# First output stage of a two-layer attention kernel: low halves on GpSimd, and the second layer's moments taken per unit

## The reference, cut to what matters

```
x = x + _L0_conv_ref(_gn(x), registers, qkv_w, qkv_b, out_w, out_b)
x = x + _L1_conv_ref(_gn(x), qkv_w, qkv_b, proj_w, proj_b, rel_pos_h, rel_pos_w)
```

## Time and profile before

| what | value |
| --- | --- |
| median of 3 runs | 3226.82 us (3225.55 to 3229.48) |
| the profiled execution | 3222.15 us, its span 3220.3 us |
| mean granted TensorE clock | 0.957 of 2.4 GHz |
| PE busy | 2905.4 us, 90% |
| DVE busy | 2476.7 us, 77% |
| ACT busy | 1861.9 us, 58% |
| POOL busy | 1902.8 us, 59% |
| DMA | 301.91 MB, mean 94 GB/s |

### The profile page before, as it was taken

One profiled execution on the slowest core, in us unless ns is written; L12 is line 12 of the kernel. 1 busy time (PEld: TensorE's weight loads), 2 busy tenths in 40 slices (PEclk: granted clock), 3 DMA queues, 4 the chain that ended last, 5 costly groups with the idle time before them and its releaser, 6 DMA issues. The chain is left out here.

```text
span 3220.3 us, 82906 instructions
## 1 busy us (share of the span) xinstructions
PE 2905.4 (90%) x34200; PEld 1874.4 (58%) x34200; DVE 2476.7 (77%) x5171; ACT 1861.9 (58%) x3434; POOL 1902.8 (59%) x1561
## 2 busy tenths in 40 slices
PE   4996999997579885999999999999999999999977
PEld 2453677774335442666666666666666666666644
DVE  6754888885666534888888888888888888888854
ACT  3333676664344432666666666666666666666655
POOL 3452555552110123777777777777777777777762
PEclk9896999998789986999999999999999999999989
DMA  3326555555437658322222222222222233332115
GB/s 142 155 89 147 135 135 141 142 140 192 143 108 215 195 131 203 63 51 52 51 52 52 51 51 51 51 52 52 51 51 51 52 61 59 58 59 54 21 42 147
DMA packets 219836, 301.91 MB, mean 94 GB/s; under 512 B 134394, under 2 KB 172884, under 8 KB 213972
## 3 DMA queue, kind: packets, MB, share of 16 engines
q1 hardware_dynamic: 219460, 296.62, 37.7%
HBM read 196.56 MB, written 92.64 MB: 90 GB/s over the span
## 5 line engine op out<-in xcount | busy, mean ns | idle before, releaser
L1746 POOL TENSOR_TENSOR fprob_low<-fprob 128x768 f16<-128x768 f32 x1008 | 1449.2, 1468 | 445.2 <-ACT fprob L1714 445.2
L1757 DVE TENSOR_REDUCE fpart_max<-fmax_acc 128x1 f32<-128x384 f32 x2592 | 1354.0, 556 | 252.0 <-PE fmax_acc L1585 235.9
L1714 ACT ACTIVATE fprob<-fscores 128x768 f32<-128x768 f32 x1296 | 1049.3, 810 | 592.5 <-PE fscores L1614 592.4
L1585 PE MATMUL fmax_acc<-fk_m,fq_m 128*128 128x384 f16 x2592 | 847.8, 327 | 32.6 <-DMA fident<-in_ident 27.6
L1612 PE MATMUL fscores<-fq_a,fk_a 128*128 128x384 f16 x2592 | 843.0, 325 | 10.6 <-DMA fk_m<-in_one_m 10.6
L1614 PE MATMUL fscores<-fq_b,fk_b 97*128 97x384 f16 x2592 | 846.9, 327 | 0.0
L1638 PE MATMUL fout_acc<-fv,fprob 128*128 128x65 f16 x7776 | 609.4, 191 | 2.5 <-POOL fprob_low L1746 2.1
L1639 PE MATMUL fout_acc<-fv,fprob_low 128*128 128x33 f16 x7776 | 593.8, 179 | 0.0
L1638 PEld LDWEIGHTS fout_acc<-fv,fprob 128*128 128x128 bf16 x7776 | 541.6, 97 | 76.5 <-POOL fprob_low L1746 5.2
L1639 PEld LDWEIGHTS fout_acc<-fv,fprob_low 128*128 128x128 f16 x7776 | 485.6, 96 | 72.5
L1131 POOL TENSOR_TENSOR prob_low<-prob 128x242 f16<-128x242 f32 (+2 forms) x360 | 250.0, 717 | 254.7 <-ACT prob L1089 252.9
(11 more groups left out here) (134 smaller groups left out, 3980.5 us busy)
## 6 DMA issues: line engine op xcount, KB each, us to landing
q_a<-q_hi SPq DMA_DIRECT2D x48, 432.0 KB, 5.7
fq_a<-q_hi SPq DMA_DIRECT2D x48, 432.0 KB, 7.6
q_a<-q_lo SPq DMA_DIRECT2D x24, 432.0 KB, 7.5
row_bias<-bias_slot SPq DMA_DIRECT2D x24, 432.0 KB, 6.8
col_bias<-bias_slot SPq DMA_DIRECT2D x72, 144.0 KB, 4.7
fq_a<-q_lo SPq DMA_DIRECT2D x24, 432.0 KB, 8.6
fq_a<-col_bias SPq DMA_DIRECT2D x24, 432.0 KB, 16.8
fq_b<-row_bias SPq DMA_DIRECT2D x24, 432.0 KB, 5.8
```

Of the source, the lines that this page charges most:

```text
L1585: nc.tensor.matmul(max_acc[:, piece_bank(g, u, j), 0:PIECE], q_m[:, b, tile * 128:(tile + 1) * 128], k_m[:, b, piece * PIECE:(piece + 1) * ...
L1714: nc.scalar.activation(prob[:, k % RING, :].rearrange("p (j n) -> p j n", j=2), scores[:, 2 * (k % 2):2 * (k % 2) + 2, 0:UNIT], ACT.Exp).t ...
L1746: engine.tensor_tensor(prob_low[:, k % RING, :], prob[:, k % RING, :], prob[:, k % RING, :].bitcast(BF16)[:, 1::2], ALU.subtract).then_inc ...
L1757: nc.vector.reduce_max(part_max[:, u % 2, j // PIECES, j % PIECES:j % PIECES + 1], max_acc[:, piece_bank(g, u, j), 0:PIECE], axis=AX.X).th ...
```

## The change

In `mix`, `normed` gets two buffers, the low halves are issued by GpSimd, in a loop over the units behind its weight step, and `normalise` keeps the multiplication alone; it waits for the low halves of two units before in place of one. After the add of unit u VectorE takes the moments of unit u - 1 (three `bn_stats`, one for each tile), and at the end those of the last unit. The tensor `stats` is made in `build` and handed to both phases; `front` for layer 1 takes no moments of its own. The number and form of the moment instructions, and what they read, stay the same.

```
 def front(nc, ctx, x, values, stats, layer, dram, sem):
...
-            for i in range(CT * B):
-                t, b = i // B, i % B
-                if layer == 0:
+            if layer == 0:
+                for i in range(CT * B):
+                    t, b = i // B, i % B
                     dve.wait_ge(x_in[i], 16)
-                for a in range(NA):
-                    at = b * TOK + a * UNIT
-                    last = nc.vector.bn_stats(stats[:, i * NA + a, :], x[:, t, at:at + UNIT])
-            link(last)
+                    for a in range(NA):
+                        at = b * TOK + a * UNIT
+                        last = nc.vector.bn_stats(stats[:, i * NA + a, :], x[:, t, at:at + UNIT])
+                link(last)
...
 def mix(nc, ctx, x, stats, layer, dram, sem):
...
-    normed = ctx.enter_context(nc.sbuf_tensor(f"normed{layer}", [128, CT, UNIT], F32))
+    normed = ctx.enter_context(nc.sbuf_tensor(f"normed{layer}", [128, 2, CT, UNIT], F32))
...
         def _(pool):
             pool.wait_ge(w_steps, 2)
             nc.gpsimd.tensor_tensor(w_lo[:, :, :], w[:, :, :], w_hi[:, :, :], ALU.subtract).then_inc(w_lo_ready, 1)
+            for u in range(UNITS):
+                pool.wait_ge(normed_hi_ready, u + 1)
+                if u >= 2:
+                    pool.wait_ge(acc_ready, (u - 1) * CT)
+                nc.gpsimd.tensor_tensor(normed_lo[:, u % 2], normed[:, u % 2], normed_hi[:, u % 2],
+                                        ALU.subtract).then_inc(normed_lo_ready, 1)
...
                 dve.wait_ge(unit_in[u % 3], 32 * (u // 3 + 1))
                 dve.wait_ge(factor_ready, u + 1)
-                if u > 0:
-                    dve.wait_ge(normed_lo_ready, u)
-                nc.vector.tensor_tensor(normed[:, :, :], factor[:, 0:CT, 0:UNIT], heads[:, u % 3],
+                if u > 1:
+                    dve.wait_ge(normed_lo_ready, u - 1)
+                nc.vector.tensor_tensor(normed[:, u % 2], factor[:, 0:CT, 0:UNIT], heads[:, u % 3],
                                         ALU.mult).then_inc(normed_ready, 1)
-                dve.wait_ge(normed_hi_ready, u + 1)
-                if u >= 2:
-                    dve.wait_ge(acc_ready, (u - 1) * CT)
-                nc.vector.tensor_tensor(normed_lo[:, u % 2], normed[:, :, :], normed_hi[:, u % 2],
-                                        ALU.subtract).then_inc(normed_lo_ready, 1)
+
+            def moments(u):
+                dve.wait_ge(added, u + 1)
+                for t in range(CT):
+                    nc.vector.bn_stats(stats[:, t * UNITS + u, :], x[:, t, u * UNIT:(u + 1) * UNIT])
...
                 nc.vector.tensor_tensor(dst, mixed[:, u % 2], dst, ALU.add).then_inc(added, 1)
+                if u >= 1:
+                    moments(u - 1)
+            moments(UNITS - 1)
...
-                nc.scalar.activation(normed_hi[:, u % 2], normed[:, :, :], ACT.Identity).then_inc(normed_hi_ready, 1)
+                nc.scalar.activation(normed_hi[:, u % 2], normed[:, u % 2], ACT.Identity).then_inc(normed_hi_ready, 1)
...
         x = whole.enter_context(nc.sbuf_tensor("x", [128, CT, ALL + REGS], F32))
+        stats = whole.enter_context(nc.sbuf_tensor("stats", [128, CT * B * NA, 6], F32))
```

More of the change, by code:

```diff
@@ L133, in split_halves, with front @@
     return halves[:, 0::2], halves[:, 1::2]
-def front(nc, ctx, x, values, layer, dram, sem):
+def front(nc, ctx, x, values, stats, layer, dram, sem):
     regs = REGS if layer == 0 else 0
@@ L157, in front @@
     normed = ctx.enter_context(nc.sbuf_tensor(f"gn_out{layer}", [128, 3, THIRD], F32))
-    stats = ctx.enter_context(nc.sbuf_tensor(f"stats{layer}", [128, CT * B * NA, 6], F32))
     chan = ctx.enter_context(nc.sbuf_tensor(f"chan{layer}", [128, CT * B, 2], F32))
@@ L1216, in _, with mix @@
             each_stage(pool, stage)
-def mix(nc, ctx, x, layer, dram, sem):
+def mix(nc, ctx, x, stats, layer, dram, sem):
     w = ctx.enter_context(nc.sbuf_tensor(f"ow{layer}", [128, CT, C], F32))
@@ L2017, in build @@
             values = first.enter_context(nc.sbuf_tensor("values", [128, HEADS, B * TILES + 1, VW], F16))
-            phase(front, x, values, 0)
+            phase(front, x, values, stats, 0)
             phase(attention, x, values, 0)
-            phase(mix, x, 0)
-        phase(front, x, None, 1)
+            phase(mix, x, stats, 0)
+        phase(front, x, None, stats, 1)
         phase(attention_full, x)
```

## The result

The changed kernel's median is 3240.01 us (10 runs), that of the kernel before 3226.55 us (10 runs): 1.0041 times as long, with a 95% interval of 1.0032 to 1.0049. The prediction was 3238, slower, with 3229 to 3247 as its range.

A forecast was written before the change was run, and what follows sets the result against it. It took TensorE (5.15 of 5.27 us a unit) and VectorE's loop as nearly equal limits. Output stage +21.3 less front 10.2 gave +11.1 us, median 3226.82 to 3237.9 (forecast 3238), range 3229 to 3247.

The forecast's parts named there:

- The loop: First output stage, per unit: add 1.13, moments 1.39, normalise to low halves 2.58, low halves 2.37; 7.47 us against 5.27.
- The rival without a wait: Output stage: the add runs beside GpSimd at full speed, loop 6.66 us, net +3.9, 3230.7 us; 12 in 100.
- The length of the stage: First output stage: nine loops of 7.47 us bring unit 11's low halves 21.3 us later.
- The six moments behind the last add: End of the output stage: 2.8 us of moments, costed at nothing because the last store covers them.
- The front: Second layer's front: without the 16.65 us moment pass, first x low halves come 10.2 us earlier, held by GpSimd's weight low halves.
- The chain to the scale factors: Second layer's front: without the moment pass, ready 14.6 us after the stage's start, or later if the group matrix lands late.
- The sum: Whole kernel: +21.3 from the output stage less 10.2 from the front, +11.1 us.
- the lower clock as a rival: Output stage: waiting TensorE drops its clock; +8 us if every other unit fell, +18 if all nine; 10 in 100.
- as before: End of the output stage: the last add starts 5.21 us after unit 11's first matmul, unchanged.
- Without a gap of its own VectorE closes the loop: Output stage before the change: VectorE's steps follow directly, TensorE waits for low halves; nearly equal limit to TensorE's 5.15 of 5.27 us.
- The rival that called VectorE's free time usable: Output stage: units overlap until TensorE sets the pace at 5.15 us; -9.7 us, 3217; 8 in 100.

The follow-up runs named there:

- run 1: Changed kernel with the second layer's moments left as a pass in the front, low halves still on GpSimd: 3237.14 us, 1.0041 times the kernel before.
- run 4: Changed kernel with the moments of unit u-1 issued before the add of unit u instead of behind it: 3224.22 us, 1.0000 times the kernel before.
- run 3: Changed kernel with a GpSimd memset of the same tile in place of the low-half subtraction: 3227.57 us, 1.0007 times the kernel before.
- run 7: run 3 with a second, longer GpSimd memset into a spare tile behind the first: 3231.2 us in a single execution.
- run 2: Changed kernel with low halves back on VectorE, moments still behind each add in the output stage: 3229.29 us, 1.0016 times the kernel before.
- run 8: run 3 with the subtraction done on GpSimd into a spare tile ahead of the memset: 3242.98 us in a single execution.
- run 6: run 5 with the second layer's weight low halves moved from GpSimd to VectorE: 3212.67 us, 0.9963 times the kernel before.
- run 5: run 2 with the moments of unit u-2 issued between normalise and low halves: 3217.47 us, 0.9972 times the kernel before.

## Why the prediction was right

*The loop.* Predicted 7.47 us a unit, measured 7.50, of the same terms: the add released by GpSimd's end, then moments, normalise, high halves, low halves. Runs 1 and 4 take the moments out of it (6.12 = 7.50 - 1.38), runs 3 and 7 the wait (6.64), run 2 both the wait and GpSimd's extra time (6.64). The rival without a wait had 6.66 for its loop and would have been right if GpSimd read nothing. That the f32 add waits was inferred from another instruction and is now shown. The Trainium skill (SBUF — State Buffer, Who interferes with whom) sets a GpSimd instruction that reads SBUF apart from one that only writes it; runs 7 and 8 agree, 1.36 us beside a write and 2.21 beside a read.

*The length of the stage.* +21.3 predicted, +21.4 measured up to unit 11's low halves. The six moments behind the last add were costed at nothing: they end at 872.36, the next stage starts at 872.98, 3.39 us after the add ended, and it was 3.38 before.

*The front.* 10.2 us predicted, 10.1 measured (34.06 to 24.00), and cut where the text put it: run 6 takes GpSimd's weights away and 2.7 us more come free. The chain to the scale factors, put at 14.6 us from the stage's start or later, took 16.34 (872.98 to 889.32): the group sums began at 876.62, when their matrix had landed, and the reciprocal waited 3.45 us for ScalarE's square root, which stood behind its work on the weights and a table load. GpSimd's end at 894.27 covered both.

*The sum.* 13.5 us by the medians (10.3 to 15.8 by the interval) against 11.1; in the profile 13.0 up to the first x low halves. Of the 1.9 between 11.1 and 13.0, 1.7 are unit 11: the last add starts 6.89 us after its first matmul (861.34 to 868.23) against 5.21 before, at a granted clock of 0.80; ten of the 27 matmuls start 0.32 us apart in place of 0.16, about 1.6 us by themselves. The text had the lower clock as a rival, with 2 us for every unit wholly at the lower level. It came about, in part: no unit was wholly slow (of the 27 from 801.36, ten were about 0.32 apart as well), and the units before lost nothing by it. In the three where the add became ready late, it still ended with GpSimd's reading, and the low halves went on every 7.50 us. The last unit has no wait for GpSimd behind it to hide in. I had put the last unit down "as before"; that step missed 1.7 us.

*A step that was wrong without harm.* "Without a gap of its own VectorE closes the loop" took two ways of nearly equal length for one. Run 5 parts them: VectorE had 1.3 us free in each unit that could be used, in the wait for the high halves, and the loop that stayed at 5.27 runs through ScalarE. The rival that called VectorE's free time usable was right in this; it was the place of the moments that forfeited it.

What stays open: why the stage began 7.7 us later in the execution profiled after. The instructions ahead of it are the same, but the shared `stats` tile moves other tiles in SBUF, and its place alone was not tried. The medians speak against a lasting cost there: they differ from the kernel before by +13.5 (changed kernel), -0.3 (run 4), -8.7 (run 5) and -13.5 us (run 6), and the traces, from the first normalise to the first x low halves, by +13.0, -0.5, -10.3 and -13.8. Run 1 alone does not fit so well (12.6 and 8.6).

## What to carry to other kernels

Free time of an engine is usable only where it lies: the same three instructions cost 1.39 us a unit behind the add and nothing ahead of it or inside a wait. Before work is moved to GpSimd, look at which VectorE instructions will become ready while GpSimd reads. Here an add with two SBUF inputs waited for the end of GpSimd's instruction (2.21 us in place of 1.36), and so did a normalise with one (5.53 us; three unhindered take 1.86); the moments, also with one, did not (before the change four of the 36 ran beside GpSimd, at the common length). The profile counts such a wait as busy time. When a pass is taken off a chain, price the next chain to the same point: here 10 of 16.65 us were to be had, until GpSimd's work on the weights was moved too.

## What the runs showed of the hardware that was not expected

On GpSimd a memset of 128x1152 f16 took 1.06 us, one of 128x2304 took 2.02, and a subtraction with the output of the first 2.36; how much of the difference is the reading was not tried apart. The lower clock came inside a stage in which TensorE waited 0.67 to 2.93 us ahead of a unit's matmuls: 0.82 in the window from 796.33 and 0.80 in the last unit, where a unit of the stage before the change had 1.00. Of the loops of 6.64 us run 2 had 0.91 from 795 to 835 us, and run 3 had 1.00 there and 0.75 in the unit from 835.15; with loops of 6.12 us or less (runs 1, 4 and 5) it was 1.00 from 795 to 835. And VectorE took the weights' low halves in 3.76 us where GpSimd needed 6.72.
